# A recurrent loop on one core: two extra products of 128 columns in each step

## Chip, core and metric

The kernel runs on one NeuronCore of a Trainium2 chip. Its engines are TensorE (PE in the rows, with PEld for its weight loads), VectorE (DVE), ScalarE (ACT), GpSimd (POOL) and SyncE (SP). The metric is the device time of one launch in microseconds (us), lower is better. The clock of TensorE that the chip granted is given as a share of its full speed: 1.00 is 2.4 GHz, 0.50 is 1.2 GHz.

## What is computed

Four layers are chained on an input of 4 x 32 x 32 tokens of 96 channels: an attention layer (L0), a bidirectional recurrent layer (L1) and two layers of a separable filter with a perceptron (L2, L3). The change lies in L1, whose core is four GRU scans over 1024 tokens each, two that run forward through the tokens and two that run backward:

```python
gx = jnp.einsum('blc,gc->blg', x, wih) + bih
def step(hprev, gxt):
    gh = hprev @ whh.T + bhh
    r = jax.nn.sigmoid(gxt[:, :h] + gh[:, :h])
    z = jax.nn.sigmoid(gxt[:, h:2 * h] + gh[:, h:2 * h])
    n = jnp.tanh(gxt[:, 2 * h:] + r * gh[:, 2 * h:])
    hn = (1.0 - z) * n + z * hprev
    return (hn, hn)
```

Here h is 96, the batch is 4, and x has 192 channels. Everything in a step depends on the step before it, so the loop is a chain of 1024 steps.

## The kernel before

The function `gru_phase` runs all four scans at once, in two groups: group u = 0 holds the two scans that go forward through the tokens, u = 1 the two that go backward. Each group has its own state `hp[u]` (h as a high and a low 16-bit part) and `hs[u]` (h in fp32), and its own banks of PSUM: `zr_bank[u, k]` for the gates z and r, and `n_bank[u, k]` for the third gate. The loop has 16 iterations of 64 steps (four chunks of T = 16 tokens); k is the chunk's parity. While the steps of one chunk read banks k, the input projections of the next chunk are written into banks 1 - k.

A gate bank is 2 gates x 2 scans x 4 images x 32 columns of fp32. The 16 tokens of a chunk fill only columns 0 to 15 of the 32; columns 16 to 31 are written and read by nothing.

The order on each engine is the order in which the code is written; each engine runs its own list and waits on semaphores. In one step TensorE does this, first for u = 0 and then for u = 1:

- line 504: eight products of 4 columns with the high part of h (after `h1_ok[u]`, which line 553 raises), then four with the high part's weights and the low part of h (after `h2_ok[u]`, which line 560 raises). The last one raises `zr_mm[u]`;
- line 511: four products of 8 columns for the third gate;
- line 480 (`projections`): four (u = 0) or five (u = 1) of the 144 products of 64 columns that make the next chunk's projections. In each step this is 9 products.

ScalarE does `gates` (sigmoid, line 592) and tanh (line 595), group 0 and then group 1. VectorE does, in this order: `before_n(0)` (line 540), `z_times_h(0)` (546), `new_h(0)` (553 and 555), `before_n(1)` (540), `low_part(0)` (560), `z_times_h(1)` (546), `new_h(1)` (553, 555), `low_part(1)` (560). So the low part of group 0's new state stands behind line 540 of group 1, which waits for group 1's gates. GpSimd copies h to the output buffer (line 612).

Ahead of the loop, 144 projection products (line 480) for the first chunk run one after the other.

Of the kernel before, what the change touches and what calls it, by code (L numbers as in the profile page):

```python
# [305 lines left out]
T = 16  # L306
# [131 lines left out]
def gru_phase(nc, inner, Y, wi, wp, unscale):  # L438
# [6 lines left out]
    with ExitStack() as c:  # L445
        def sb(n, s, d=F): return c.enter_context(nc.sbuf_tensor("g_" + n, s, d))
        def sem(n): return c.enter_context(semaphore(nc, "g_" + n))
# [7 lines left out]
        zr_bank = {(u, k): c.enter_context(nc.psum_tensor(f"g_zr{u}{k}", [128, 2, 2, NB, 2 * T], F))  # L455
                   for u in range(2) for k in range(2)}
# [12 lines left out]
        def projections(pe, chunk, k, items):  # L469

            for d, g, half, i in items:
                u, K, (px, pw) = d // 2, (96, 98)[half], PRODUCTS[i]

                at = T + chunk * T if u == 0 else L - chunk * T
                o = n_terms[u, k][:, (d % 2) * NB:(d % 2 + 1) * NB, 2, :] if g == 2 else \
                    zr_bank[u, k][:, 1 - g, d % 2, :, 0:T]
                x = inner[0:K, half, px, :, bass.ds(at, T)]

                first = d % 2 == 0 and half == 0 and g != 1 and i == 0
                pe.matmul(o, wi[0:K, half, pw, d * NG + g, :], x, start=first, stop=False, skip_group_check=True)  # L480
# [5 lines left out]
        @block.tensor  # L486
        def _(pe):
            pe.wait_ge(init, 4)
            projections(pe, 0, 0, items)
            with pe.Fori(0, NC // UNROLL) as i:  # L490
                for kk in range(UNROLL):
                    k = kk % 2
                    for t in range(T):
                        s = (i * UNROLL + kk) * T + t
                        for u in range(2):
                            at = column(u, t)


                            for e, ok, parts in ((1, h1_ok, 2), (0, h2_ok, 1)):
                                pe.wait_ge(ok[u], s + 1)  # L500
                                for g in range(2):
                                    for d in range(2):
                                        for part in range(parts):
                                            mm = pe.matmul(zr_bank[u, k][:, 1 - g, d, :, at],  # L504
                                                           wp[0:97, part, (2 * u + d) * NG + g, :],
                                                           hp[u][0:97, d * NB:(d + 1) * NB, e], start=False,
                                                           stop=(e == 0), skip_group_check=True)
                            mm.then_inc(zr_mm[u], 1)
                            for d in range(2):
                                for part in range(2):  # L510
                                    mm = pe.matmul(n_terms[u, k][:, d * NB:(d + 1) * NB, 0:2, at],  # L511
                                                   wp[0:97, part, (2 * u + d) * NG + 2, :],
                                                   hp[u][0:97, d * NB:(d + 1) * NB, :],
                                                   start=False, stop=(part == 1), skip_group_check=True)
                            mm.then_inc(n_and_gates[u], 1)

                            q = 2 * t + u
                            projections(pe, i * UNROLL + kk + 1, 1 - k,
                                        items[q * len(items) // (2 * T):(q + 1) * len(items) // (2 * T)])

        @block.vector
        def _(ve):
# [727 lines left out]
def gru_block(nc, d, x, v, mean96, eps5):  # L1250
    with ExitStack() as outer:
        z = outer.enter_context(nc.sbuf_tensor("s_z", [C, 2, N], F))
        with ExitStack() as mid:
            y = mid.enter_context(nc.sbuf_tensor("s_y", [C, ND, N], F))
            with ExitStack() as ctx:
                wi, wp, unscale = gru_weights(nc, ctx, d["L1_wih"], d["L1_whh"])

                inner = ctx.enter_context(nc.sbuf_tensor("s_inner", [C + 2, 2, 3, NB, L + 2 * T], BF))
                with ExitStack() as c2:
                    w_in = c2.enter_context(nc.sbuf_tensor("s_w_in", [C, 4 * C], F))  # L1260
                    xn = y[:, 2, :]
                    load(nc, "s", [(w_in[:, :], d["L1_w_in"])])
                    with semaphore(nc, "s_cleared") as cleared, nc.Block() as block:
                        @block.gpsimd
                        def _(po):
                            po.memset(inner[0:C, :, :, :, 0:T], 0.0)
                            po.memset(inner[0:C, :, :, :, L + T:L + 2 * T], 0.0)
                            po.memset(inner[C:C + 2, 1, 0, :, :], 1.0)

                        @block.vector  # L1270
                        def _(ve):
                            ve.memset(inner[C:C + 2, 1, 1:3, :, :], 0.0)
                    layernorm(nc, "s_ln", [x], [xn], [v["L1_ln_g"][:, :]], [v["L1_ln_b"][:, :]], mean96,
                              eps5[:, :])

                    def spread(act, m, b, psum):
                        if m < 2:
                            return act.activation(y[:, m, cols(b)], psum, ACT.Copy)
                        return act.activation(z[:, m - 2, cols(b)], psum, ACT.Silu)
                    project(nc, "s_in", [xn], lambda s, m: w_in[:, m * C:(m + 1) * C], 4, C, spread, "scalar")  # L1280
                split_bf16(nc, "s_split", [(y[:, h, cols(b)], y[:, 2 + h, cols(b)],
                                            [inner[0:C, h, p, b, T:T + L] for p in range(3)])
                                           for b in range(NB) for h in range(2)])
                gru_phase(nc, inner, y, wi, wp, unscale)
# [634 lines left out]
```

## Time and profile before

| what | value |
|---|---|
| time, median of 3 runs | 3518.51 us (3518.45 to 3518.85) |
| the profiled execution's own time | 3515.43 us |
| its span, first to last instruction | 3513.3 us |
| recurrent loop in it | about 1348 to 3013 us |
| busy over the span: PE, DVE, ACT, POOL | 87%, 72%, 52%, 29% |
| mean granted clock of TensorE over the span | 0.701 |

The profiled execution is 3.1 us below the median, and 2.1 us of it lie outside the span. Busy times of PE overlap, because products are pipelined: a product's row says when it was started and how long it took to its end, and the next one starts before that end. The distance from one start to the next is what TensorE needs for a product; it is read from the start times of consecutive rows.

### The profile page before, as it was taken

Reading aid. Unit: us, or ns where it says so; the run is one execution under the profiler, and the core shown is the slowest. Engines: PE = TensorE matmul, PEld = TensorE weight load, DVE = VectorE, ACT = ScalarE, POOL = GpSimd, SP = SyncE. Lnnn points to the kernel's source line nnn. Section 1 sums busy time; section 2 is a strip of 40 time slices with the busy share of each in tenths; the row PEclk is TensorE's granted clock in tenths of the full one; section 3 lists DMA queues with packets and bytes.
Section 4 is the critical chain, followed back from the end, with each engine's and each line's share of the span. In section 5 each row is a group of like instructions: output and inputs, shape, how many; then the busy total and the mean of one; then the engine's idle time right before and its main releaser. Section 6 shows DMA issues by size and latency. Waiting matters only on the chain. (4 is left out here: it accounts for less than half of the span.)

```text
span 3513.3 us, 136148 instructions
## 1 busy us (share of the span) xinstructions
PE 3044.4 (87%) x50244; PEld 2300.0 (65%) x50244; DVE 2527.1 (72%) x12097; ACT 1814.5 (52%) x5570; POOL 1031.7 (29%) x2514
## 2 busy tenths in 40 slices
PE   5459999999958667999999999999999999568987
PEld 1136666666613226888988888988888898445654
DVE  4639999999956337777777777777777777668882
ACT  1249999999903035444544444544444454234443
POOL 0028777877700001222222222222222222100000
PEclk9669999999968875555555555555555555579899
DMA  1243333333220000000000000000000000000000
GB/s 34 84 139 110 109 99 100 111 109 112 84 83 0 16 2 3 5 5 5 4 5 5 5 5 5 5 5 5 5 5 5 5 5 5 13 1 1 1 5 14
DMA packets 54609, 116.11 MB, mean 33 GB/s; under 512 B 12314, under 2 KB 19802, under 8 KB 53693
## 3 DMA queue, kind: packets, MB, share of 16 engines
q1 hardware_dynamic: 37104, 53.42, 5.4%
q0 software_dynamic: 13824, 50.34, 4.0%
q8 instruction: 400, 6.55, 0.8%
q10 hardware_dynamic: 2956, 3.15, 0.4%
q14 instruction: 325, 2.65, 0.3%
HBM read 84.06 MB, written 22.81 MB: 30 GB/s over the span
## 5 line engine op out<-in xcount | busy, mean ns | idle before, releaser
L504 PE MATMUL g_zr<-g_hp,g_wp 97*128 97x4 f16 x24576 | 1077.0, 171 | 49.3 <-issue 49.0
L504 PEld LDWEIGHTS g_zr<-g_hp,g_wp 97*128 97x128 f16 x24576 | 951.2, 108 | 156.3 <-issue 51.3
L612 POOL COPY s_y<-g_hs 96x8 f32 x2048 | 401.0, 196 | 1357.1 <-DVE g_hs L555 1357.1
L595 ACT ACTIVATE g_e<-g_tn 96x8 f32<-96x8 f32 x2048 | 439.3, 214 | 555.5 <-DVE g_tn L540 555.5
L480 PE MATMUL g_zr<-s_inner,g_wi 96*128 (+2 forms) x6240 | 586.0, 234 | 49.0 <-issue 26.8
L553 DVE TENSOR_TENSOR_SCAN g_hp<-g_gates,g_e 96x16 f16<-96x16 f32 x2048 | 383.9, 187 | 324.2 <-ACT g_e L595 218.3
L592 ACT ACTIVATE g_gates<-g_zr 96x16 f32<-96x16 f32 x2048 | 400.3, 195 | 305.7 <-PE g_zr L504 304.7
L868 DVE CUSTOM_DVE_ANT_0 a_negated<-a_scores,a_mask 128x1024 f32<-128x1024 f32 x384 | 468.1, 1219 | 84.7 <-DMA a_mask<-in_L_mask 44.0
L511 PE MATMUL g_n<-g_hp,g_wp 97*128 97x8 f16 x8192 | 520.2, 174 | 0.0
L894 ACT ACTIVATE a_probs<-a_negated,a_negmax 128x1024 f32<-128x1024 f32 x384 | 442.3, 1152 | 25.3 <-DVE a_negmax L868 15.5
L540 DVE TENSOR_TENSOR_SCAN g_tn<-g_gates,g_n 96x24 f32<-96x24 f32 x2048 | 386.3, 189 | 82.1 <-ACT g_gates L592 82.1
L816 PEld LDWEIGHTS a_turned<-a_ident,a_probs 128*128 128x128 f32 x3072 | 357.1, 141 | 94.6 <-ACT a_probs L894 4.0
L816 PE MATMUL a_turned<-a_ident,a_probs 128*128 128x128 f32 x3072 | 413.3, 276 | 0.8 <-ACT a_probs L894 0.4
L480 PEld LDWEIGHTS g_zr<-s_inner,g_wi 96*128 96x128 bf16 (+1 forms) x6240 | 373.5, 117 | 53.1 <-issue 29.1
L511 PEld LDWEIGHTS g_n<-g_hp,g_wp 97*128 97x128 f16 x8192 | 376.8, 104 | 0.0
L560 DVE TENSOR_TENSOR g_hp<-g_hs,g_hp 96x8 f16<-96x8 f32 x2048 | 341.7, 167 | 34.8
L555 DVE TENSOR_TENSOR_SCAN g_hs<-g_gates,g_e 96x16 f32<-96x16 f32 x2048 | 338.0, 165 | 0.0
L546 DVE SCALAR_TENSOR_TENSOR g_e<-g_gates,g_hs 96x8 f32<-96x8 f32 x2048 | 312.5, 153 | 0.0
L480 PE MATMUL g_n<-s_inner,g_wi 96*128 (+2 forms) x3120 | 297.7, 237 | 0.0
L765 POOL TENSOR_SCALAR a_term<-r_vpad,r_lepe_w 96x1024 f32<-96x1024 f32 x96 | 274.9, 2864 | 8.2
L851 DVE COPY a_probs_t<-a_turned 128x512 f32<-128x512 f32 x384 | 263.4, 686 | 0.8 <-PE a_turned L816 0.8
L853 ACT ACTIVATE a_probs_t<-a_turned 128x512 f32<-128x512 f32 x384 | 227.5, 592 | 44.0 <-PE a_turned L816 34.0
(319 smaller groups left out, 3278.1 us busy)
## 6 DMA issues: line engine op xcount, KB each, us to landing
a_mask<-in_L_mask POOLq DMA_DIRECT2D x96, 512.0 KB, 5.5
a_k<-k_rows SPq DMA_DIRECT2D x96, 144.0 KB
q_rows<-r_q_parts SPq DMA_DIRECT2D x12, 576.0 KB, 7.2
k_rows<-r_k_parts SPq DMA_DIRECT2D x12, 576.0 KB, 7.2
a_q<-q_rows SPq DMA_DIRECT2D x96, 72.0 KB
o_parts<-a_o_sb SPq DMA_DIRECT2D x384, 18.0 KB
o_part<-o_parts SPq DMA_DIRECT2D x32, 192.0 KB
out_x<-x SPq DMA_DIRECT2D x4, 384.0 KB, 3.0
```

Source lines behind the costliest of these rows:

```text
L480: pe.matmul(o, wi[0:K, half, pw, d * NG + g, :], x, start=first, stop=False, skip_group_check=True)
L504: mm = pe.matmul(zr_bank[u, k][:, 1 - g, d, :, at], wp[0:97, part, (2 * u + d) * NG + g, :], hp[u][0:97, d * NB:(d + 1) * NB, e], start=False,
L511: mm = pe.matmul(n_terms[u, k][:, d * NB:(d + 1) * NB, 0:2, at], wp[0:97, part, (2 * u + d) * NG + 2, :], hp[u][0:97, d * NB:(d + 1) * NB, :],
L540: ve.tensor_tensor_scan(flat(tn[u][:, :, :]), flat(gates[u][:, :, 0:6:2]), flat(n_terms[u, k][0:C, :, :, column(u, t)]), 0.0, ALU.mult, AL ...
L553: ve.tensor_tensor_scan(flat(hp[u][0:C]), keep, flat(e1[u][:, :, :]), 0.0, ALU.mult, ALU.subtract).then_inc(h1_ok[u], 1)
L560: ve.tensor_tensor(hp[u][0:C, :, 0], hs[u][:, t % 2, :, 1], hp[u][0:C, :, 1], ALU.subtract).then_inc(h2_ok[u], 1)
L592: act.activation(gates[u][:, :, 3:5].rearrange("p c g -> p g c"), zr, ACT.Sigmoid, scale=to_gate).then_inc(n_and_gates[u], 1)
L595: act.activation(e1[u][:, :, 0], tn[u][:, :, 2], ACT.Tanh, scale=to_tanh).then_inc(n_and_zh[u], 1)
L612: po.tensor_copy(yv[:, 2 * u:2 * u + 2, :, bass.ds(token, 1)], h.unsqueeze(3)).then_inc(y_ok[u], 1)
L816: mm = pe.transpose(turned_bank(half, m)[:, k, :], probs[m % 2][:, kt * 128:(kt + 1) * 128], ident[:, :])
L868: ve.tensor_tensor_reduce(out=negated[m % 4][:, :], in0=scores[m % 2][:, :], in1=masks[half][c][:, :], scale=-1.0, scalar=3.0e38, op0=ALU.add,
L894: act.activation(probs[m % 2][:, :], negated[m % 4][:, :], ACT.Exp, bias=negmax[m % 4][:, :], scale=-1.0).then_inc(expd, 1)
```

## The change

Behind the projections of group 0, in every step, TensorE does two more products. Each has the same stationary weights (`wi[0:96, 0, 0, 0, :]`), 128 moving columns (4 images x 32 tokens of `inner`) and writes 2 scans x 4 images x 16 columns in the unused half of `zr_bank[0, 1 - k]`, once for each gate. Nothing reads what they write; no wait and no semaphore is added. That is 2048 products in the loop, and 2048 loads of weights.

```diff
@@ -517,6 +517,11 @@
                             q = 2 * t + u
                             projections(pe, i * UNROLL + kk + 1, 1 - k,
                                         items[q * len(items) // (2 * T):(q + 1) * len(items) // (2 * T)])
+                            if u == 0:
+                                for half in range(2):
+                                    pe.matmul(zr_bank[u, 1 - k][:, half, :, :, T:2 * T], wi[0:96, 0, 0, 0, :],
+                                              inner[0:96, 0, 0, :, T:3 * T], start=False, stop=False,
+                                              skip_group_check=True)
```

On TensorE, one step of the first chunk stands like this in the kernel before (in `g_zr01` the digits are u and k; `g_hp0` is group 0's state):

```order
584 L504 MATMUL g_zr00<-g_hp0,g_wp 128x4 x12
585 L511 MATMUL g_n00<-g_hp0,g_wp 128x4x2 x4
586 L480 MATMUL g_zr01<-s_inner,g_wi 128x4x16 x2
587 L480 ISA
588 L480 MATMUL g_zr01<-s_inner,g_wi 128x4x16 x2
589 L504 MATMUL g_zr10<-g_hp1,g_wp 128x4 x12
590 L511 MATMUL g_n10<-g_hp1,g_wp 128x4x2 x4
591 L480 MATMUL g_zr01<-s_inner,g_wi 128x4x16 x5
```

The same step after the change:

```order
585 L504 MATMUL g_zr00<-g_hp0,g_wp 128x4 x12
586 L511 MATMUL g_n00<-g_hp0,g_wp 128x4x2 x4
587 L480 MATMUL g_zr01<-s_inner,g_wi 128x4x16 x2
588 L480 ISA
589 L480 MATMUL g_zr01<-s_inner,g_wi 128x4x16 x2
590 L522 MATMUL g_zr01<-s_inner,g_wi 128x8x16 x2
591 L504 MATMUL g_zr10<-g_hp1,g_wp 128x4 x12
592 L511 MATMUL g_n10<-g_hp1,g_wp 128x4x2 x4
```

The two products of line 522 stand between group 0's projections and group 1's twelve gate products. VectorE's order, which the change leaves alone, is this in each step:

```order
562 L540 SCALAR_TENSOR_TENSOR g_tn0<-g_gates0,g_n00 96x24
564 L546 SCALAR_TENSOR_TENSOR g_e10<-g_gates0,g_hs0 96x8
565 L553 SCALAR_TENSOR_TENSOR g_hp0<-g_gates0,g_e10 96x16
566 L555 SCALAR_TENSOR_TENSOR g_hs0<-g_gates0,g_e10 96x16
567 L540 SCALAR_TENSOR_TENSOR g_tn1<-g_gates1,g_n10 96x24
568 L560 TENSOR_TENSOR g_hp0<-g_hs0,g_hp0 96x8
569 L546 SCALAR_TENSOR_TENSOR g_e11<-g_gates1,g_hs1 96x8
570 L553 SCALAR_TENSOR_TENSOR g_hp1<-g_gates1,g_e11 96x16
571 L555 SCALAR_TENSOR_TENSOR g_hs1<-g_gates1,g_e11 96x16
572 L560 TENSOR_TENSOR g_hp1<-g_hs1,g_hp1 96x8
```

Nothing moved here; the rows show that line 560 of group 0 stands right behind line 540 of group 1.

## Rows read from the trace of the kernel before

**Rows 1.** Waits inside 1500 to 2900: waiter, releaser, us in total, times, longest.

```profile
ACT g_gates L592 <- PE g_zr L504: 252.7, 860, 3.9
```

**Rows 2.** 1360 to 1440: length, busy us (count) of each engine, clock, DMA.

```profile
core 0: us, PE busy (x) PEld busy (x) DVE busy (x) ACT busy (x) POOL busy (x), PEclk, DMA share, GB/s
1360.00:1440.00 80.00, 80.00 (x2120) 74.41 (x2118) 61.81 (x517) 40.88 (x207) 20.37 (x104) 0.50 0.02 4
```

**Rows 3.** Timeline of one step, from 2001.5: start us, us, engine, line, operation.

```profile
2001.53 0.18 DVE L540 TENSOR_TENSOR_SCAN g_tn<-g_gates,g_n 96x24 f32<-96x24 f32 x1
...
2001.64 0.17 DVE L560 TENSOR_TENSOR g_hp<-g_hs,g_hp 96x8 f16<-96x8 f32 x1
...
2002.00 0.25 PE L511 MATMUL g_n<-g_hp,g_wp 97*128 97x8 f16 x4
...
2002.10 0.38 PE L480 MATMUL g_zr<-s_inner,g_wi 98*128 x4
2002.17 0.20 ACT L592 ACTIVATE g_gates<-g_zr 96x16 f32<-96x16 f32 x1 [0.22 <-PE g_zr L504]
...
2002.29 0.50 PE L504 MATMUL g_zr<-g_hp,g_wp 97*128 97x4 f16 x12
2002.29 0.17 DVE L560 TENSOR_TENSOR g_hp<-g_hs,g_hp 96x8 f16<-96x8 f32 x1
2002.40 0.20 DVE L540 TENSOR_TENSOR_SCAN g_tn<-g_gates,g_n 96x24 f32<-96x24 f32 x1
...
2002.64 0.25 PE L511 MATMUL g_n<-g_hp,g_wp 97*128 97x8 f16 x4
...
2002.82 0.20 ACT L592 ACTIVATE g_gates<-g_zr 96x16 f32<-96x16 f32 x1
2002.83 0.35 PE L480 MATMUL g_n<-s_inner,g_wi 96*128 x3
...
2003.08 0.18 DVE L540 TENSOR_TENSOR_SCAN g_tn<-g_gates,g_n 96x24 f32<-96x24 f32 x1
2003.12 0.16 PEld L504 LDWEIGHTS g_zr<-g_hp,g_wp 97*128 97x128 f16 x3
...
2003.19 0.17 DVE L560 TENSOR_TENSOR g_hp<-g_hs,g_hp 96x8 f16<-96x8 f32 x1
```

**Rows 4.** Timeline of TensorE ahead of the loop: projections one after the other.

```profile
1344.91 1.47 PE L480 MATMUL g_zr<-s_inner,g_wi 96*128 96x64 bf16 x24
1346.19 0.83 PE L480 MATMUL g_n<-s_inner,g_wi 96*128 96x64 bf16 x12
```

**Rows 5.** TensorE by stretch: length, busy us (count), granted clock, DMA share, GB/s.

```profile
1341.20:1347.60 6.40, 6.40 (x123) 0.50 0.01 3
1347.70:1351.00 3.30, 3.10 (x106) 1.00 0.02 5
1351.20:1446.00 94.80, 94.75 (x2509) 0.50 0.02 5
700.00:720.00 20.00, 20.00 (x151) 1.00 0.44 148
```

**Rows 6.** Timeline of TensorE in the attention, from 700: products of 512 columns.

```profile
700.08 0.60 PE L786 MATMUL a_scores<-a_k,a_q 96*128 96x512 bf16 x2
700.52 1.04 PE L816 MATMUL a_turned<-a_ident,a_probs 128*128 128x128 f32 x8
```

**Rows 7.** Timeline of the loop's first step, from 1349.4, at full clock.

```profile
1349.46 0.19 DVE L553 TENSOR_TENSOR_SCAN g_hp<-g_gates,g_e 96x16 f16<-96x16 f32 x1 [0.20 <-ACT g_e L595]
...
1350.20 0.28 PE L480 MATMUL g_zr<-s_inner,g_wi 98*128 x4
...
1350.35 0.54 PE L504 MATMUL g_zr<-g_hp,g_wp 97*128 97x4 f16 x12
1350.41 0.17 DVE L560 TENSOR_TENSOR g_hp<-g_hs,g_hp 96x8 f16<-96x8 f32 x1
...
1351.00 0.19 DVE L553 TENSOR_TENSOR_SCAN g_hp<-g_gates,g_e 96x16 f16<-96x16 f32 x1 [0.20 <-ACT g_e L595]
```

## The prediction, made before the run

> **What bounds the kernel now.** The chain of waits on the page is no help here: it follows the last work, the filter layers, and covers about an eighth of the span. The loop is read from three other views of its steady part. The waits first [rows 1]: from 1500 to 2900 ScalarE's sigmoid waited 860 times for the gate products, about once in a step, although it runs twice in a step, once for each group. So only one of the two groups waits; the other finds its inputs ready. The timeline of one step says which [rows 3]: group 0's sigmoid at 2002.17 has the wait behind it, group 1's at 2002.82 has none. The length of a step comes from a count [rows 2]: VectorE has five instructions per group and step, and 517 of them in 80 us are 51.7 steps, so a step takes 1.547 us, and 1024 of them 1584 us; the rest of the loop's 1665 us is spent elsewhere, and I leave it as it is.
>
> Group 0's own recurrence sets that 1.547. Its low part (line 560) starts at 2001.64 and again at 2003.19, 1.55 later, and everything between (four gate products, sigmoid, line 540, tanh, lines 553 and 555) follows at once. Group 1 rides inside it with little room. TensorE looks full, 94.75 of 94.80 us [rows 5], but that is overlap of pipelined products. By starts, group 1's five projections begin at 2002.75 (three of them at 2002.83, at 53 ns each) and are done at 2002.99, while group 0's next weight load starts at 2003.12 [rows 3]: 0.13 us of real idle time per step. Some 0.05 more lies between group 0's first eight products and its last four, which wait for line 560. The clock is 0.50, 1.2 GHz, throughout.
>
> **The change, part by part.**
>
> *Price of an added product.* The trace of before has no 128-column product in 16 bits at low clock. The nearest is the 64-column product of line 480: 24 of them from 1344.91 to 1346.19 [rows 4], 53.3 ns each, that is 0.83 ns for a column, which is one column a cycle at 1.2 GHz. So 128 columns are taken at 107 ns, two at 0.213 us. The bound from below: if two products of 128 columns cost no more than two of 64, 0.107. From above: 0.213 plus two starts of a gate product, 0.35/12 = 0.029 each [rows 3], if their weight loads weren't hidden, 0.27. I take 0.213, since the 64-column products hide their weight loads in the same place. At full clock two products of 512 columns start within 0.44 us [rows 6], 0.43 ns per column, so the two added ones would cost 0.11.
>
> *Where it falls.* Not in TensorE's idle time, which lies at the end of a step, ahead of group 0. The two stand directly ahead of group 1's gate products, and there TensorE doesn't rest: projections at 2002.10, gate products at 2002.29. So group 1's gates come 0.21 later, and the question is who waits for group 1. VectorE does: line 540 of group 1 waits for the gates, and behind it in VectorE's list stands line 560 of group 0, the low part on which group 0's recurrence rests. That closes a loop through both groups, and its length decides. From the starts in rows 3:
> - line 560 of group 0 to the third-gate products (2001.64 to 2002.00): 0.36
> - these to the projections (to 2002.10): 0.10
> - four projections, to group 1's gate products (to 2002.29): 0.19
> - twelve gate products, to line 511 (2002.29 to 2002.64): 0.35. Group 1's own low part (line 560 at 2002.29) is ready at 2002.51 and doesn't delay them
> - last gate product to sigmoid (2002.64 to 2002.82): 0.18
> - sigmoid to line 540, read from group 0, where VectorE was free (2002.17 to 2002.40): 0.23
> - line 540 of group 1 to line 560 of group 0 (2001.53 to 2001.64): 0.11
>
> The sum is 1.52 us, 0.027 under the step. That is all the room there is, and the rows agree: line 540 of group 1 could have started at 2002.82 + 0.23 = 2003.05 and started at 2003.08. With the two products the loop is 1.52 + 0.213 = 1.733 us, and it takes over from group 0's recurrence as the bound. The step grows by 0.186 us, and 1024 steps by **190 us**.
>
> *Does another link break first?* Group 0's first eight products come after group 1's projections: counted from line 560 at 0, group 1's line 511 starts at 1.00 + 0.213 = 1.21, its projections end 0.11 + 0.24 later at 1.56, and eight products take 0.24, to 1.80; the low part of the next step is ready for them at 1.733 + 0.22 = 1.95. No delay. ScalarE and the copy on GpSimd have idle time in every step. Everything outside the loop is untouched: 0.
>
> *The sum.* Against its own time the profiled execution goes from 3515.4 to 3705.6. The median of the runs lies 3.1 above that execution, so 3708.7, rounded to **3709 us**, 5.4% slower. Ends of this case: if VectorE can start line 560 earlier behind line 540 and part of the added time is hidden (0.14 per step), 3518.5 + 143 = 3662. If the whole 0.213 shows, 3518.5 + 218 = 3737.
>
> **A rule that says otherwise.** The rows: TensorE ran the projections ahead of the loop back to back at 0.50, then the granted clock was 1.00 from 1347.7 to 1351.0, and within the loop's first three steps it fell to 0.50 again and stayed there [rows 5]. The Trainium skill, "TensorE: Matmul & The Clock Gate", section "What's actually happening", says why filler might help: "the default state is throttled, and activity releases the throttle." By that rule the two products are activity, and the time would be the first rival's; by the rows as they stand, it is the sum above.
>
> **Rivals.**
>
> *The added columns bring the full clock (faster).* Mechanism: with the filler TensorE is granted 1.00 in the loop as it was at 1348. The price is in the loop's first step, which ran at full clock [rows 7]: 1349.46 to 1351.00, 1.54 us against 1.547. Full clock gives back only 0.007 us, since group 0's recurrence runs mostly over VectorE and ScalarE. The two products would cost nothing there: group 0's projections start at 1350.20 and are done by 1350.32, the added ones by 1350.43 instead of a start at 1350.35, but group 1's last four products wait anyway for line 560 (1350.41 + 0.22 = 1350.63), and eight products fit before it. So 1024 x 0.007 = 7 us less, **3511 us**; it decides if the clock is 1.00 for nearly the whole loop. Against it: the clock fell at 1351 although the steps before held the dense end of the projections, and at full clock the same products leave more gaps, not fewer. Chance 7%.
>
> *The clock goes up and down.* A share of the steps at 1.54 and the rest at 1.733; with half of each about **3610 us**. Chance 4%. Here the fall at 1351 speaks for it, and 95 us without a rise after it speak against it.
>
> *The groups slide apart and TensorE's idle time takes the products (no change).* TensorE idles 0.13 + 0.05 = 0.18 us per step, close to the 0.213. If group 1 could run later by 0.2 us without holding group 0, only 0.03 would be left: **3518 to 3550 us**. It would need line 560 of group 0 not to wait behind line 540 of group 1; VectorE's list has it there. Chance 4%.
>
> *The products aren't issued as written,* for instance merged or dropped since nothing reads them: the order of the changed program has them on line 522 in each step. 1%, 3518.
>
> **How the numbers follow.** The forecast (low clock, the loop through both groups) has 84%, of which about 80 lie between 3660 and 3740; those are the range's ends, since the cases left out hold 20. A measurement of this kernel can tell about 0.2%, 7 us, from no change. Faster by more than that: the first rival, a little over half of whose chance lies beyond 7 us, and unforeseen gains, 6%. Within it: the rest of that rival, the last one and part of the third, 6%. Slower: 88%.
>
> **What the changed kernel's profile would show.** The granted clock in the loop: 0.50 for the forecast, 1.00 for the first rival, a mean between for the second. A step: 1.73 us by the count of VectorE's instructions. Waits: line 540 of group 1 now waits for the sigmoid in every step, and line 560 of group 0 starts right behind it. Starts of line 522 and of the gate products behind it: 0.21 from the end of group 0's projections to group 1's first gate product. I would be wrong if the clock rises, or if line 560 of group 0 starts at its old distance from line 553.

## Result and profile after

The changed kernel took 3686.3 us at the median of 4 runs (3680.5 to 3693.5), against 3518.5 us before; the ratio is 1.048, with a 95% interval of 1.0465 to 1.0492. That is 168 us slower. The profiled execution is the longest of the four, 3693.5 us with a span of 3691.3, 178 above that of before. Its lines after 519 have numbers 5 higher than before: line 545 is `before_n` (540), 558 and 560 are `new_h` (553, 555), 565 is `low_part` (560), 597 and 600 are sigmoid and tanh; 522 is the added product.

TensorE by stretch: length, busy us (count), granted clock, DMA share, GB/s. The first row is the end of the projections ahead of the loop and the loop's first steps, the other two are the loop.

```profile
1348.10:1354.80 6.70, 6.44 (x206) 1.00 0.01 2
1355.00:1446.00 91.00, 90.99 (x2288) 0.50 0.02 4
1500.00:2900.00 1400.00, 1332.06 (x33463) 0.50 0.02 5
```

The clock fell within the first steps and stayed at 0.50, as in [rows 5]. All engines from 1360 to 1440, the stretch of [rows 2]:

```profile
core 0: us, PE busy (x) PEld busy (x) DVE busy (x) ACT busy (x) POOL busy (x), PEclk, DMA share, GB/s
1360.00:1440.00 80.00, 80.00 (x2017) 76.16 (x2015) 58.90 (x468) 38.16 (x187) 19.35 (x93) 0.50 0.02 4
```

VectorE's 468 instructions are 46.8 steps, 1.709 us each, against 1.547, which is 0.162 more in this stretch. Over the whole loop, with the ends of its iterations left out, line 555 of group 0 (560 in the changed kernel) starts every 1.551 us before and every 1.719 after. That is 0.168 us, or 172 us over 1024 steps, of the 178 by which the two profiled executions differ. The waits from 1500 to 2900, the stretch of [rows 1]:

```profile
ACT g_gates L597 <- PE g_zr L504: 272.1, 1147, 3.9
```

The sigmoid now waits 1147 times, against 860, although the stretch holds fewer steps: group 1's gates are late too. The view counts only waits above 0.15 us; in the trace ScalarE sits idle 0.15 us ahead of group 1's sigmoid in the mean, and not at all in the kernel before. VectorE stands idle for them as well, which the page's groups show (the last part has the idle time before the group, then how much of it the row's releaser ended). The idle time of the row grows by 74 us, 0.07 per step. Before and after, `before_n`:

```profile
L540 DVE TENSOR_TENSOR_SCAN g_tn<-g_gates,g_n 96x24 f32<-96x24 f32 x2048 | 386.3, 189 | 82.1 <-ACT g_gates L592 82.1
```

```profile
L545 DVE TENSOR_TENSOR_SCAN g_tn<-g_gates,g_n 96x24 f32<-96x24 f32 x2048 | 409.0, 200 | 156.2 <-ACT g_gates L597 81.7
```

One step of the changed kernel, in the order of [rows 3] (start us, us, engine, line):

```profile
2000.13 0.18 DVE L565 TENSOR_TENSOR g_hp<-g_hs,g_hp 96x8 f16<-96x8 f32 x1
...
2000.49 0.25 PE L511 MATMUL g_n<-g_hp,g_wp 97*128 97x8 f16 x4
...
2001.75 0.20 DVE L545 TENSOR_TENSOR_SCAN g_tn<-g_gates,g_n 96x24 f32<-96x24 f32 x1
...
2001.87 0.15 DVE L565 TENSOR_TENSOR g_hp<-g_hs,g_hp 96x8 f16<-96x8 f32 x1
...
2002.20 0.25 PE L511 MATMUL g_n<-g_hp,g_wp 97*128 97x8 f16 x4
...
2002.31 0.37 PE L480 MATMUL g_zr<-s_inner,g_wi 98*128 x4
...
2002.50 0.40 PE L522 MATMUL g_zr<-s_inner,g_wi 96*128 96x128 bf16 x2
...
2002.69 0.51 PE L504 MATMUL g_zr<-g_hp,g_wp 97*128 97x4 f16 x12
...
2003.06 0.25 PE L511 MATMUL g_n<-g_hp,g_wp 97*128 97x8 f16 x4
...
2003.12 0.19 DVE L558 TENSOR_TENSOR_SCAN g_hp<-g_gates,g_e 96x16 f16<-96x16 f32 x1 [0.21 <-ACT g_e L600]
...
2003.23 0.19 ACT L597 ACTIVATE g_gates<-g_zr 96x16 f32<-96x16 f32 x1
...
2003.46 0.20 DVE L545 TENSOR_TENSOR_SCAN g_tn<-g_gates,g_n 96x24 f32<-96x24 f32 x1
...
2003.58 0.17 DVE L565 TENSOR_TENSOR g_hp<-g_hs,g_hp 96x8 f16<-96x8 f32 x1
```

In the kernel before, line 553 of group 0 stands here ahead of its line 560 at 2003.19 [rows 3]:

```profile
2002.88 0.19 DVE L553 TENSOR_TENSOR_SCAN g_hp<-g_gates,g_e 96x16 f16<-96x16 f32 x1 [0.21 <-ACT g_e L595]
```

This is the loop through both groups. In both kernels group 0's low part starts 0.11 to 0.12 behind line 540 (545) of group 1. What changed is that line 545 now waits for its gates and holds the low part back: from line 558 to line 565 of group 0 it is 0.46 us (2003.12 to 2003.58), where it was 0.31 from 553 to 560. Group 1's low part, which waits behind nobody's gates, keeps its 0.31 in both kernels. Everything from one start of line 565 of group 0 to the next follows without rest: 0.33 + 0.11 + 0.19 + 0.19 + 0.37 + 0.17 + 0.23 + 0.12 = 1.71.

### The profile page after: what moved, and what is told of

Same layout as the page of the kernel before. It is cut to its first block and busy times, and to the rows that moved or that the text cites. A ratio compares the mean times of both kernels' runs of the same rounds, so it can differ in the third digit from the quotient of the medians.

```text
span 3691.3 us, 140244 instructions
## 1 busy us (share of the span) xinstructions
PE 3210.9 (87%) x52292; PEld 2489.2 (67%) x52292; DVE 2599.2 (70%) x12097; ACT 1841.2 (50%) x5570; POOL 1040.3 (28%) x2514
## 5 line engine op out<-in xcount | busy, mean ns | idle before, releaser
L504 PE MATMUL g_zr<-g_hp,g_wp 97*128 97x4 f16 x24576 | 1180.0, 172 | 61.2 <-issue 51.7
L504 PEld LDWEIGHTS g_zr<-g_hp,g_wp 97*128 97x128 f16 x24576 | 1065.3, 110 | 146.0 <-issue 54.0
L617 POOL COPY s_y<-g_hs 96x8 f32 x2048 | 411.2, 201 | 1519.2 <-DVE g_hs L560 1519.2
L545 DVE TENSOR_TENSOR_SCAN g_tn<-g_gates,g_n 96x24 f32<-96x24 f32 x2048 | 409.0, 200 | 156.2 <-ACT g_gates L597 81.7
L522 PE MATMUL g_zr<-s_inner,g_wi 96*128 96x128 bf16 x2048 | 410.7, 304 | 0.0
L565 DVE TENSOR_TENSOR g_hp<-g_hs,g_hp 96x8 f16<-96x8 f32 x2048 | 327.0, 160 | 34.8
```

The costliest lines, as they stand in the source:

```text
L504: mm = pe.matmul(zr_bank[u, k][:, 1 - g, d, :, at], wp[0:97, part, (2 * u + d) * NG + g, :], hp[u][0:97, d * NB:(d + 1) * NB, e], start=False,
L522: pe.matmul(zr_bank[u, 1 - k][:, half, :, :, T:2 * T], wi[0:96, 0, 0, 0, :], inner[0:96, 0, 0, :, T:3 * T], start=False, stop=False, skip_ ...
L545: ve.tensor_tensor_scan(flat(tn[u][:, :, :]), flat(gates[u][:, :, 0:6:2]), flat(n_terms[u, k][0:C, :, :, column(u, t)]), 0.0, ALU.mult, AL ...
L617: po.tensor_copy(yv[:, 2 * u:2 * u + 2, :, bass.ds(token, 1)], h.unsqueeze(3)).then_inc(y_ok[u], 1)
```

## Experiments

All kernels below are timed beside the kernel before on the same chip, whose median was 3516.9 to 3519.0 us. Each median is of 4 runs, of 10 for e3 and of 2 for e5 and e6. The step is read from the count of VectorE's instructions in the stretch 1360 to 1440, ten to a step.

| kernel | us, median (interval of the ratio) | step, us | clock in the loop |
|---|---|---|---|
| before | 3517 to 3519 | 1.547 | 0.50 |
| the change | 3686.3 (1.0465 to 1.0492) | 1.709 | 0.50 |
| e3, products behind group 1 | 3526.5 (1.0012 to 1.0031) | 1.553 | 0.50 |
| e4, one product of 128 columns | 3588.3 (1.0159 to 1.0211) | 1.600 | 0.50 |
| e7, two products of 64 columns | 3573.0 (1.0133 to 1.0167) | 1.600 | 0.50 |
| e8, two products of 16 columns | 3534.4 (1.0032 to 1.0066) | 1.566 | 0.50 |
| e2, VectorE's order alone | 3723.4 (1.0562 to 1.0600) | 1.758 | 0.50 |
| e1, VectorE's order and the products | 3727.7 (1.0573 to 1.0611) | 1.758 | 0.50 |
| e6, 4 fillers of 256 columns | 4117.6 (1.1678 to 1.1725) | 1.556 | 1.00 in that stretch, then 0.50 |
| e5, 6 fillers of 256 columns | 3784.5 (1.0733 to 1.0776) | 1.735 | 1.00 in that stretch and mostly |

### The same products in another place

The edit against the changed kernel:

```diff
-                            if u == 0:
+                            if u == 1:
                                 for half in range(2):
-                                    pe.matmul(zr_bank[u, 1 - k][:, half, :, :, T:2 * T], wi[0:96, 0, 0, 0, :],
+                                    pe.matmul(zr_bank[0, 1 - k][:, half, :, :, T:2 * T], wi[0:96, 0, 0, 0, :],
```

> Both added products moved behind group 1's projections, at the end of a step, where TensorE idled 0.13 us in the kernel before. Theory: 0.13 of the 0.21 falls in idle time, group 0's first eight products start 0.07 later, and these had 0.05 before the low part was due, so 0.02 to 0.03 per step is left: 3550 us (3530 to 3570). Rival, what counts is the work on TensorE and not its place: 3686.

It took 3526.5 us, 9.5 above before: the same 2048 products of 128 columns cost 5.7% of what they cost in the change's place. The count of the stretch:

```profile
1360.00:1440.00 80.00, 80.00 (x2212) 79.64 (x2209) 61.68 (x515) 40.47 (x207) 19.90 (x104) 0.50 0.02 5
```

515 instructions are 51.5 steps, 1.553 us. The expectation was still too high, by 0.02 to 0.03 per step; TensorE's order there shows where they went:

```profile
2000.21 0.43 PE L480 MATMUL g_zr<-s_inner,g_wi 96*128 x5
2000.45 0.40 PE L522 MATMUL g_zr<-s_inner,g_wi 96*128 96x128 bf16 x2
2000.65 0.51 PE L504 MATMUL g_zr<-g_hp,g_wp 97*128 97x4 f16 x12
2001.01 0.25 PE L511 MATMUL g_n<-g_hp,g_wp 97*128 97x8 f16 x4
```

Group 0's gate products follow the added ones at once and need 0.36 us, with almost no wait for the low part between them. The late start of the first eight is paid for by the wait that stood before the last four. By its starts TensorE now does a whole step without rest (from group 0's first gate product at 1999.09 to the next at 2000.65), and the step of 1.553 less the 0.213 of the added products leaves 1.34 us for its own list. So it had idled 0.21 us per step in the kernel before, not the 0.18 of the prediction, and the two products just fit. The place was nearly free because they fit; what a third would cost here was not measured. In the change's place TensorE has the same work, so it is the place that costs. The rival that work on TensorE counts wherever it stands falls.

### How much work, and how much room

One product instead of two, against the changed kernel:

```diff
-                                for half in range(2):
+                                for half in range(1):
```

> One added product of 128 columns instead of two, in the same place. Theory: the loop through both groups with 0.107 us instead of 0.213, so 1.713 - 0.107 = 1.606 us per step against 1.547: 3579 us (3570 to 3600, the upper end by the sum of the prediction, 1.52 + 0.107). If the price were simply proportional to the products, half of 168: 3602.

Two products of half the columns, against the changed kernel:

```diff
-                                    pe.matmul(zr_bank[u, 1 - k][:, half, :, :, T:2 * T], wi[0:96, 0, 0, 0, :],
-                                              inner[0:96, 0, 0, :, T:3 * T], start=False, stop=False,
+                                    pe.matmul(zr_bank[u, 1 - k][:, half, :, :, T:T + T // 2], wi[0:96, 0, 0, 0, :],
+                                              inner[0:96, 0, 0, :, T:2 * T], start=False, stop=False,
```

> Two added products in the change's place, but of 64 columns each instead of 128. If the price goes by columns, as the sum had it, the two cost 0.107 us together and the kernel takes what it took with one product of 128 columns, 3588 us (3575 to 3600). If it goes by products, it stays near 3686.

Two products of 16 columns, `T:T + 2` in the bank and `T:T + 4` in `inner`:

> Two added products of 16 columns each in the change's place. Products of 4 and 8 columns start 0.027 us apart, so the two take 0.053 us. It measures the room in the loop through both groups, which the prediction put at 0.027 us. With that room the step grows by 0.026: 3545 us. From the steps of 1.713 us with 0.213 added and 1.600 with 0.107 the loop without products would be 1.49 to 1.50, a room of about 0.05: 3518 to 3525 us. If each added product had a price of its own beyond its columns, it would be above 3560.

The rows of 1360 to 1440 for e4, e7 and e8:

```profile
1360.00:1440.00 80.00, 80.00 (x2102) 77.18 (x2100) 60.71 (x500) 40.89 (x200) 19.75 (x100) 0.50 0.02 4
```

```profile
1360.00:1440.00 80.00, 80.00 (x2150) 77.18 (x2148) 60.84 (x500) 40.65 (x200) 19.51 (x100) 0.50 0.02 4
```

```profile
1360.00:1440.00 80.00, 80.00 (x2197) 75.94 (x2195) 61.19 (x511) 41.35 (x205) 19.85 (x103) 0.50 0.02 5
```

The same 128 columns as one or as two products give the same step, 1.600 us: between 64 and 128 columns the price goes by columns, and a product has none of its own beyond them. The steps are 1.566, 1.600 and 1.709 us with 0.053, 0.107 and 0.213 us of added products. From 0.107 to 0.213 the step grows by 0.109, one for one. The loop without products would be 1.709 - 0.213 = 1.496 or 1.600 - 0.107 = 1.493, a room of 0.05 under the 1.547, but 1.566 - 0.053 = 1.513 by the smallest dose, a room of 0.03. Both values of the last expectation miss: 3534 us lies between them. What varies is one link of the loop, the time of group 0's low part. The pages' rows of it (both groups together; the second number behind the bar is the mean in ns) for the kernel before, the change, e8 and e4:

```profile
L560 DVE TENSOR_TENSOR g_hp<-g_hs,g_hp 96x8 f16<-96x8 f32 x2048 | 341.7, 167 | 34.8
L565 DVE TENSOR_TENSOR g_hp<-g_hs,g_hp 96x8 f16<-96x8 f32 x2048 | 327.0, 160 | 34.8
L565 DVE TENSOR_TENSOR g_hp<-g_hs,g_hp 96x8 f16<-96x8 f32 x2048 | 331.2, 162 | 34.8
L565 DVE TENSOR_TENSOR g_hp<-g_hs,g_hp 96x8 f16<-96x8 f32 x2048 | 316.8, 155 | 34.8
```

Group 1's low part keeps 0.167 us in all of them. Group 0's takes 0.167 before, and in the mean 0.152 in the change, 0.156 in e8 and 0.142 in e4. With the mean steps over the whole loop, ends of iterations left out, and the low part set back to 0.167, the loop without products is 1.719 - 0.213 + 0.015 = 1.521 for the change, 1.567 - 0.053 + 0.011 = 1.525 for e8 and 1.603 - 0.107 + 0.025 = 1.521 for e4. So the loop is the 1.52 of the prediction at every dose, and its room the predicted 0.03; the rest is the shorter low part.

e4 and e7 have one step length but 15 us between their medians. A stretch that holds an iteration's end, 1600 to 1700, has 583 instructions of VectorE in e4 and 592 in e7:

```profile
1600.00:1700.00 100.00, 93.55 (x2450) 90.05 (x2451) 71.04 (x583) 47.64 (x234) 23.25 (x116) 0.50 0.02 5
```

```profile
1600.00:1700.00 100.00, 94.68 (x2546) 91.19 (x2542) 72.01 (x592) 48.16 (x236) 23.53 (x119) 0.50 0.02 5
```

Nine instructions are 0.9 steps. Over all 15 ends of an iteration the starts of line 560 show e4 to need 1.0 us more at each, 16 us together, while the two profiled loops are 14 us apart. So in the profiled executions the difference lies where the loop branches back, and why that took longer in e4 stays open. The two kernels were also timed in different rounds, and the intervals of their ratios overlap.

### VectorE's order

In e1 the change is kept and group 0's low part is put ahead of group 1's `before_n`; e2 does the same in the kernel before.

```diff
-                        before_n(1, k, t, s)
                         low_part(0, t, s)
+                        before_n(1, k, t, s)
```

> The changed kernel with both added products, and in VectorE's list group 0's low part (line 560 of before) put ahead of group 1's line 540. Theory of the loop through both groups: group 0's low part no longer waits for group 1's gates, so the loop of 1.71 us per step is gone. Group 1 then runs about 0.22 us later, which leaves TensorE a gap between group 0's projections and group 1's gate products, and the two products (0.21 us) fit it: about 1.56 us per step, 3535 us (3520 to 3570). Rival, the products lie on the path by TensorE's order alone, whatever VectorE's list: it stays at 3686.

> The kernel before with the same new order in VectorE's list and no added products, the control for the run above. Two steps of group 0 by way of group 1 (line 560, 540, tanh, 553 of group 1, its products and projections, then group 0's next gate products) come to 3.11 us, 1.556 per step against 1.547: 3527 us (3515 to 3545). If the new order were itself a gain that hides the price of the products, it would be below 3510.

Both expectations missed by nearly 200 us in the time: 3727.7 and 3723.4. The new order is itself a loss, larger than the change. VectorE in e2:

```profile
2000.69 0.19 DVE L553 TENSOR_TENSOR_SCAN g_hp<-g_gates,g_e 96x16 f16<-96x16 f32 x1 [0.21 <-ACT g_e L595]
2000.80 0.17 DVE L555 TENSOR_TENSOR_SCAN g_hs<-g_gates,g_e 96x16 f32<-96x16 f32 x1
2001.00 0.17 DVE L560 TENSOR_TENSOR g_hp<-g_hs,g_hp 96x8 f16<-96x8 f32 x1
2001.08 0.19 DVE L540 TENSOR_TENSOR_SCAN g_tn<-g_gates,g_n 96x24 f32<-96x24 f32 x1
...
2001.55 0.19 DVE L553 TENSOR_TENSOR_SCAN g_hp<-g_gates,g_e 96x16 f16<-96x16 f32 x1 [0.22 <-ACT g_e L595]
...
2002.45 0.19 DVE L553 TENSOR_TENSOR_SCAN g_hp<-g_gates,g_e 96x16 f16<-96x16 f32 x1 [0.21 <-ACT g_e L595]
```

From one group's line 553 through its low part (0.31), the other group's line 540 (0.08) and tanh to the other's line 553 (0.47) is 0.86 us, and the same way back is 0.90 (2001.55 to 2002.45). I had followed only the half from group 0 to group 1 and not seen that `before_n(0)` stands behind `low_part(1)` in the list already, so that the swap closes a second loop, on VectorE and ScalarE alone, of 1.76 us.

The pair still tells something on the change. In e2 TensorE idles between group 0's projections and group 1's gate products; in e1 the two products fill it:

```profile
2001.46 0.38 PE L480 MATMUL g_zr<-s_inner,g_wi 98*128 x4
2001.80 0.55 PE L504 MATMUL g_zr<-g_hp,g_wp 97*128 97x4 f16 x12
```

```profile
2001.39 0.37 PE L480 MATMUL g_zr<-s_inner,g_wi 98*128 x4
2001.57 0.40 PE L522 MATMUL g_zr<-s_inner,g_wi 96*128 96x128 bf16 x2
2001.77 0.52 PE L504 MATMUL g_zr<-g_hp,g_wp 97*128 97x4 f16 x12
```

0.34 us from projections to gate products without them, 0.38 with them, the same step of 1.758, and 4 us between the medians, about as much as the spread of each. The same products, in the same place of TensorE's list, cost 168 us in the change and next to nothing here, where TensorE idles at that place. More the pair can't say: its step of 1.758 us is longer than the 1.71 of the change, and would hide a loop of that length whichever way it ran. An order of VectorE's list that opens the loop through both groups and closes no other was not run.

### Would the full clock have paid?

Both kernels have no added products of the change, but fillers of 128 rows and 256 columns from a zeroed tensor, three behind each group's projections in e5, one behind group 0's and three behind group 1's in e6. The edit of e5 (e6 has `(1, 3)` in its place; the tensor and its memset are left out here):

```diff
+                            for _ in range((3, 3)[u]):
+                                pe.matmul(zr_bank[0, 1 - k][:, :, :, :, T:2 * T].rearrange("p g d b t -> p (g d b) t"),
+                                          filler[:, 256:384], filler[:, 0:256], start=False, stop=False,
+                                          skip_group_check=True)
```

> The kernel before with three added products of 256 columns behind each group's projections, from a zeroed tensor of 128 rows of their own (1536 columns in a step instead of the change's 256). It asks the first rival's question with much more filler: does the clock stay at 1.00 in the loop? If it does: the loop through both groups at full clock, 1.70 us per step with 0.32 us of filler behind group 0, 3675 us (3600 to 3750). If the clock falls to 0.50: TensorE's own work, 1.37 + 1.28 = 2.65 us per step, is the bound, about 4640 us (4500 to 4750). My theory says nothing on the clock; the rival's view is that more filler brings the full clock.

> As the run above, with one product of 256 columns behind group 0 and three behind group 1, where TensorE idles (1024 columns in a step). If the clock stays at 1.00, 0.11 us behind group 0 is absorbed and 0.32 behind group 1 nearly so: 1.54 to 1.56 us per step, 3515 to 3530 us, no gain over before, since the loop's first step at full clock took 1.54 us. If it falls to 0.50: 1.37 + 0.85 = 2.22 us per step, about 4210 us (4100 to 4300).

Neither case of e6's expectation is the whole of it: the clock did both. The engines by stretch in e6, columns as above:

```profile
1360.00:1440.00 80.00, 80.00 (x2316) 77.11 (x2313) 62.01 (x514) 40.08 (x206) 19.91 (x103) 1.00 0.02 5
1460.00:1540.00 80.00, 80.00 (x1649) 70.84 (x1645) 48.40 (x368) 29.92 (x146) 14.10 (x73) 0.50 0.01 3
1500.00:2900.00 1400.00, 1360.22 (x27903) 1200.52 (x27902) 815.69 (x6205) 508.19 (x2481) 239.79 (x1241) 0.50 0.02 4
```

The first iteration of the loop ran at full clock to its end. There TensorE stood still for 2.9 us with no wait that the profile shows, as the timeline of e6 has it by the idle time behind the row (line 504 has number 505 here):

```profile
1452.87 0.48 PE L505 MATMUL g_zr<-g_hp,g_wp 97*128 97x4 f16 x12 [2.90 <-issue]
```

At that point the clock fell, and it never came back: 36.8 steps in 80 us are 2.17 us a step, near the 2.22 worked out for low clock, and the time is 4118 us. At full clock, though, 51.4 steps in 80 us are 1.556 us a step, with 1024 filler columns in it. So in that stretch the filler was nearly free, and the full clock gave nothing back: 1.556 is not under the 1.547 of the kernel before. In e5 the clock fell at an iteration's end too and came back each time:

```profile
1360.00:1440.00 80.00, 80.00 (x2175) 76.36 (x2172) 59.01 (x461) 37.58 (x185) 17.94 (x92) 1.00 0.02 4
1464.50:1487.00 22.50, 21.06 (x378) 17.94 (x378) 10.17 (x78) 6.23 (x32) 3.17 (x17) 0.50 0.01 3
1488.50:1560.00 71.50, 71.50 (x1946) 68.27 (x1944) 52.63 (x413) 33.66 (x165) 15.98 (x82) 1.00 0.02 4
1500.00:2900.00 1400.00, 1350.95 (x34987) 1268.10 (x34983) 953.10 (x7443) 606.77 (x2977) 289.95 (x1488) 0.93 0.02 5
```

Its step at full clock is 1.735 us (1.70 was expected, with 0.32 us of filler behind group 0), and with the slow stretches it makes 3785 us, above the 3750 that I had as the upper end. The changed kernel itself ran its first steps at full clock, and its line 565 of group 0 there:

```profile
1351.38 0.17 DVE L565 TENSOR_TENSOR g_hp<-g_hs,g_hp 96x8 f16<-96x8 f32 x1
...
1352.92 0.17 DVE L565 TENSOR_TENSOR g_hp<-g_hs,g_hp 96x8 f16<-96x8 f32 x1
...
1354.47 0.17 DVE L565 TENSOR_TENSOR g_hp<-g_hs,g_hp 96x8 f16<-96x8 f32 x1
```

1.54 and 1.55 us per step with the two products in: what the first rival said of their price and of what the full clock gives. The fillers differ from the change's products in more than their number (128 rows for 96, zeros for numbers, another tensor), so e5 and e6 do not tell which of these made the clock differ.

## Why the prediction held, point by point

**The bound.** Group 0's own recurrence sets the step of the kernel before, and TensorE's high busy share is no bound. e3 shows it: 0.21 us of work more on TensorE per step, and the step grows by 0.006. The idle time was put at 0.18 us per step and is 0.21.

**The clock.** It stayed at 0.50, as the forecast had it. The first rival's price was right (no more than 0.007 us per step in the full clock). Its argument against was drawn from the clock's fall at 1351 alone and did not reach to other fillers: in e5 the mean granted clock from 1500 to 2900 was 0.93. In the changed kernel it was 0.50.

**The loop through both groups.** This was the mechanism, and its consequences came as worked out: line 540 of group 1 waits for its gates, holds line 560 of group 0 back by 0.15 us, and the price is one for one in columns once the room is used. The direct test by VectorE's order failed as a prediction, since the swap closes another loop. What carries the point is the trace of the changed kernel, where every link follows the one before without rest, with e3 and the doses of e8, e4 and e7, from which the same loop of 1.52 us comes out each time.

**The terms.** Forecast 1.733 us, measured 1.719 in the mean, with single steps of 1.71 and 1.74. Against the rows of the changed kernel: line 560 to the third-gate products 0.36, measured 0.33; to the projections 0.10, measured 0.11; projections 0.19 and added products 0.213 and gate products 0.35, together 0.75, measured 0.19 + 0.19 + 0.37 = 0.75; to the sigmoid 0.18, measured 0.17; to line 540 0.23, measured 0.23; to line 560 0.11, measured 0.12. So the mis-sized term is the first, the way through the low part. The low part took 0.15 us at 2001.87, and the term was 0.33 and the step 1.71; it took 0.18 at 2000.13, and the term was 0.36 and the step 1.74. Over the loop it is the same: the steps that start with a low part under 0.15 us have a mean of 1.710, those with 0.17 and more 1.740. The mean term is 0.339, against 0.352 in the kernel before, from which the prediction had read a single one of 0.36. Why the same instruction takes 0.14 to 0.18 us is not settled. It is not its place in the list, since it stood as close behind line 540 before and took 0.167.

**The sum.** 190 us were forecast and 168 measured at the median. The profiled execution, the longest of the four, has 178, of which 172 lie in the steps. Of the 18 us in the steps that the forecast has too many, 14 are the loop (1.733 forecast, 1.719 measured) and 4 the base step (1.547 from one stretch, 1.551 over the whole loop). Another 6 us of the 178 lie outside the steps, where the forecast had none. The other three runs are 3 to 13 us shorter than the profiled one and have no trace, so the last 10 us to the median stay open.

**The rivals.** The groups did not slide apart so that TensorE's idle time takes the products: group 1 can't run later without holding line 560 of group 0. The same idle time takes them at once when they stand where it lies, in e3.

## What to carry to other kernels

In a recurrence over several engines the question to an added instruction is not whether its engine has idle time, but whether the idle time lies where the instruction stands; the same work cost 9.5 us at the end of a step, where it just fitted, and 168 us in its middle. Look for loops that run through the lists of other engines: a wait for one group's result holds whatever stands behind it in the same list, here the other group's state. Filler for the clock's sake pays only if steps at full clock are shorter in the trace at hand; here the first steps, which ran at full clock anyway, said beforehand that they are not.

## What was not expected of the hardware

In e6 one and the same step ran at full clock up to a pause and at half of it ever after. TensorE kept the full clock there for the whole first iteration, about 100 us, lost it at a pause of 2.9 us, and had it nowhere in the 1.4 ms shown of the same steps afterwards. In e5 it lost it at the same kind of pause and regained it, in the case shown after some 23 us. And one and the same VectorE instruction of 96 x 8 elements took 0.15 us in one step and 0.18 in the next; it is a link of the loop, where 0.03 us are more than 1% of the step.
